# Routing the first image's tokens between the matmuls of the second image's convolution (convolution mixer and mixture of experts, float32)

## What is computed

```python
def _branch(x, w, d):                      # d in (1, 4, 8, 12), nine taps each
    f = conv(x, w, dilation=d); f = softmax over the nine taps, per pixel
    return sum over taps k of shift_k(x, d) * f[k]
def _L0_conv_ref(x, ...):
    cat = concatenate([x] + [_branch(x, w, d) for w, d in ...], axis=1)   # 1280 channels
    y = w_proj @ cat + b_proj
    return relu(_group_norm(y, gamma, beta))
def _moe(tokens, router_w, w1, b1, w2, b2):
    probs = softmax(tokens @ router_w.T)
    rw, re = top_k(probs, 2); rw = rw / rw.sum(-1)
    out = tokens
    for e in range(8):
        out = out + combine[:, e:e + 1] * (gelu(tokens @ w1[e] + b1[e]) @ w2[e] + b2[e])
    return out
x = x + _L0_conv_ref(_ln_c(x), ...)
t = _to_tokens(x)                          # 18432 tokens
t = t + _L0_ffn_ref(_ln_t(t), ...)
```

## Time and profile before

| | us |
|---|---|
| median of 3 runs (lowest to highest) | 2617.31 (2616.59 to 2630.79) |
| the profiled execution | 2616.45 |
| its span | 2614.6 |
| A0, A1 (17 to 247, 700 to 936) | 230, 236 |
| C0, C1 (313 to 700, 1002 to 1393) | 387, 391 |
| R (1393 to 1843) | 450 |
| experts (1843 to 2388) | 545 |
| output (2388 to 2615) | 227 |

### The profile page before, as it was taken

The page is one execution under the profiler, slowest core; times in us unless marked ns, Lnnn a source line. Parts: engine busy times, 40 slices in busy tenths (PEclk is TensorE's granted clock), DMA queues, the critical chain, the costliest instruction groups (busy, mean ns, idle before and its releaser), DMA issues.

```text
span 2614.6 us, 61081 instructions
## 1 busy us (share of the span) xinstructions
PE 2046.2 (78%) x20292; PEld 1918.8 (73%) x20293; DVE 1624.7 (62%) x4238; ACT 1187.8 (45%) x2441; POOL 1026.5 (39%) x1390
## 2 busy tenths in 40 slices
PE   5887699999688867999994766750799999995332
PEld 4777499999678757999993766650799999994222
DVE  3554475666555545656665867663577899885644
ACT  4654233333256533333333544440577777773211
POOL 4444012233234411223320677777455566563000
PEclk9999599999899977999996655555899999997555
DMA  4332156677433214656766897753566555555887
GB/s 122 91 88 68 47 174 157 158 179 176 123 85 85 79 43 132 170 142 170 174 160 186 277 325 264 257 189 131 164 195 206 172 162 159 150 158 177 289 296 271
DMA packets 328031, 434.91 MB, mean 166 GB/s; under 512 B 86586, under 2 KB 253114, under 8 KB 326778
## 3 DMA queue, kind: packets, MB, share of 16 engines
q1 hardware_dynamic: 273618, 315.07, 42.9%
q0 software_dynamic: 41024, 97.10, 10.7%
q10 hardware_dynamic: 13200, 20.19, 2.1%
HBM read 278.46 MB, written 159.94 MB: 168 GB/s over the span
## 4 chain that ended last, share of the span: by engine, by line
PE 46%; DMA 17%; POOL 15%; issue 10%; DVE 5%; ACT 4%; DVEq 2%; SPq 1%; POOLq 0%; ACTq 0%
PE ps_y L381 16%; POOL expert_in L1786 8%; DMA expert_out<-e_out,dest 7%; PE ps L381 6%; POOL taps L1752 6%; PE ps_o L854 6%; PE ps_a L381 5%; PE ps_b L790 5%; DMA o_y<-expert_out 3%; DMA o_acc<-res_scratch 2%; ACT g_rows L1059 2%; PE ps_f L762 2%; DMA expert_in<-c_ln,pos 2%; PE ps_o L841 1%; PE ps_x L967 1%
## 5 line engine op out<-in xcount | busy, mean ns | idle before, releaser
L381 PE MATMUL ps_y<-cat_hi,wp 128*128 128x288 f32 x2048 | 469.5, 305 | 1.8 <-DVE cat_lo L1370 1.8
L1774 POOL DMA_DIRECT2D patches<-rows_scratch x352 | 194.8, 598 | 651.5 <-PE ps_o L854 492.4
L1809 POOL DMA_INDIRECT expert_out<-e_out,dest x304 | 310.3, 1021 | 237.4 <-DMA expert_out<-e_out,dest 117.4
L1786 POOL DMA_INDIRECT expert_in<-c_ln,pos x288 | 294.4, 1022 | 186.8 <-DVE pos L1515 92.1
L381 PEld LDWEIGHTS ps_y<-cat_hi,wp 128*128 128x128 f32 x2048 | 343.2, 189 | 2.0 <-DVE cat_lo L1370 2.0
L1137 ACT ACTIVATE cat_hi<-ps_o 128x288 fp32r<-128x288 f32 (+1 forms) x576 | 200.1, 386 | 252.9 <-PE ps_o L854 164.2
L381 PE MATMUL ps_y<-cat_lo,wp 128*128 128x288 f32 x1024 | 301.4, 294 | 0.0
L1370 DVE SCALAR_TENSOR_TENSOR cat_lo<-ps_o,cat_hi 128x288 fp32r<-128x288 f32 (+1 forms) x576 | 219.4, 419 | 129.8 <-ACT cat_hi L1137 129.6
L1752 POOL TENSOR_TENSOR taps<-taps,g_rows 96x108 f32<-96x108 f32 (+1 forms) x432 | 200.7, 494 | 242.2 <-ACT g_rows L1059 238.5
L381 PE MATMUL ps<-e_hi,w_now 128*128 128x256 f32 x1216 | 243.8, 284 | 1.2 <-issue 1.1
L381 PE MATMUL ps<-w,h_hi 128*128 x1216 | 234.5, 291 | 5.6 <-DVE h_lo L1658 5.6
(11 more groups left out here) (181 smaller groups left out, 4774.1 us busy)
## 6 DMA issues: line engine op xcount, KB each, us to landing
e_x<-expert_in SPq DMA_DIRECT2D x152, 260.0 KB
o_y<-expert_out SPq DMA_DIRECT2D x48, 768.0 KB, 5.3
patches<-rows_scratch SPq DMA_DIRECT2D x160, 192.0 KB
patches<-rows_scratch SPq DMA_DIRECT2D x256, 108.0 KB
patches<-rows_scratch SPq DMA_DIRECT2D x192, 112.0 KB
x_in<-in_x SPq DMA_DIRECT2D x48, 384.0 KB, 3.3
rows_scratch<-rows_st SPq DMA_DIRECT2D x48, 384.0 KB, 3.1
y_scratch<-y_acc SPq DMA_DIRECT2D x16, 1152.0 KB, 11.6
```

The costliest lines, as they stand in the source:

```text
L381: mm = eng.matmul(out, lhs[p], rhs[q], start=start and n == 0, stop=stop and n == 2)
L1774: pool.dma_start(patch_target(s, n), patch_source(m, s, n)).then_inc(patch_pooled[s % RING], 16)
L1786: pool.indirect_dma_start(out=xs_dram, out_offset=bass.IndirectOffsetOnAxis(ap=at, axis=0), in_=c_ln[:, v, k // TT, k % TT], in_offset=Non ...
L1809: pool.indirect_dma_start(out=ys_dram, out_offset=bass.IndirectOffsetOnAxis(ap=at, axis=0), in_=e_out[:, u, j], in_offset=None).then_inc(e ...
```

## The change

Image 0's part of R is done inside C1, one tile of 128 tokens at a time, in **slots** between the units; R then handles only image 1, 12 pairs. Slots lie at unit n = 1 of each step (at n = 2 in kind 1 of the classes), and at n = 5 of kind 3 as well: 79 slots, of which 72 take a tile and 12 rank a pair. To make room:

- `ps_b` has one bank instead of two, and a band matrix is made in two halves (`band(s, 0)`, `band(s, 1)`), the second one at n = 1 of the step before, in both images. The bank that is free, `ps_k`, takes one transposed tile, six tiles' router products and the counts.
- The ring of patches has three buffers instead of four (RING), in both images. In C1 POOL begins 6 of 18 patch loads in kind 3 and none in strips; SP begins the others.
- SP also loads image 0's x and y in C1 (24 blocks, 48 loads) and stores 72 tiles of the residual; POOL does image 0's additions x + y (24) and its 144 scatters, three per step.
- The router products are taken from the tile before normalisation (x as the stationary operand), and mean and deviation are put in on VectorE with the sum of the router's rows.
- Six constants are loaded at the program's start and not in R; image 0's group norm is done at the start of A1, image 1's in R. In R the expert weights, biases and fills are begun after the second pair's loads and not halfway.
- EARLY goes from 30 to 28.

```diff
-RING = 4
+RING = 3
-EARLY = 30
+EARLY = 28
...
-            ps_b = psum(r1, "ps_b", [128, 2, 512])
+            ps_b = psum(r1, "ps_b", [128, 512])
+            ps_k = psum(r1, "ps_k", [128, 512])
...
+        slot_ticks = []
+        for s_ in range(1, STEPS):
+            first = 2 if kind(s_) == 1 and s_ > UNITS1 else 1
+            slot_ticks += [unit(s_) + first] + ([unit(s_) + 5] if kind(s_) == 3 else [])
+        slot_of_tick = {u: k for k, u in enumerate(slot_ticks)}
...
+        ROUTE_AT, RANK_AT = TP - 1, TP + 2
...
-        def second_queue(s, n):
-
+        def second_queue(m, s, n):
+
+            if m:
+                return n % 3 == 2 and kind(s) == 3
             return n % 2 == 1 if kind(s) == 3 else kind(s) == 0 and n >= 6
```

SP in C1, and in R:

```diff
+                if m:
+                    sp.wait_ge(y_stored, 16 * 8)
+                    load_block(0)
+                    load_block(1)
+                blocks, kept = 2, 0
                 for s in range(STEPS):
+                    while m and blocks < ITILES // TT and slot_step(3 * blocks - 4) + 3 <= s:
+                        load_block(blocks)
+                        blocks += 1
+                    while m and kept < ITILES and slot_step(kept) + 4 <= s:
+                        store_residual(kept)
+                        kept += 1
                     load_patches(s)
...
+            load(0, 0)
+            load(1, 1)
+            sp.dma_start(etiles[:], a["k_etiles"]).then_inc(consts_in, 16)
+            sp.dma_start(w_stage[:].rearrange("p e c -> p (e c)"), a["w1"]).then_inc(w_loaded, 16)
```

PE:

```diff
+                def turn_tile(t):
+
+                    j, k = divmod(t, TT)
+                    pe.wait_ge(r_x1, j + 1)
+                    for c in range(CC):
+                        pe.transpose(ps_k[:, c * 128:(c + 1) * 128], r_x[:, j % 2, c, k * 128:(k + 1) * 128], ident[:])
+                    for c in range(CC):
+                        mm = pe.matmul(ps_k[:, 256 + t % TP * E:256 + (t % TP + 1) * E], r_x[:, j % 2, c, k * 128:(k + 1) * 128],
+                                       router[:, c], start=c == 0, stop=c == CC - 1)
+                    mm.then_inc(r_tok, 1)
...
+                def slot(k):
+
+                    after(pe, r_resd, min(k, ITILES))
+                    after(pe, r_read, min(k // TP, CPAIRS))
+                    after(pe, r_based, max(0, min((k - RANK_AT + TP - 1) // TP, CPAIRS)))
+                    if k >= RANK_AT and (k - RANK_AT) % TP == 0 and k < RANK_AT + ITILES:
+                        rank_pair((k - RANK_AT) // TP)
+                    if k < ITILES:
+                        turn_tile(k)
...
                 for s in range(STEPS):
                     if s + 1 < STEPS:
-                        band(s + 1)
+                        band(s + 1, 0)
                     for n in range(CC * parts(s)):
                         branch(s, n // parts(s), n % parts(s))
+                        k = slot_at(m, s, n)
+                        if k is not None:
+                            slot(k)
                         if s and n in (1, 3):
                             project(s - 1, n // 2, 0)
                             project(s - 1, n // 2, 1)
+                        if n == 1 and s + 1 < STEPS:
+                            band(s + 1, 1)
```

ScalarE (norm_tile normalises one tile from ps_k into r_ln, deviate is the square root of one tile's variance, relu_block group norm and ReLU of a block of three tiles):

```diff
                     for n in range(CC * parts(s)):
                         cat(s, n // parts(s), n % parts(s))
+                        if n == 1 and s + 1 < STEPS:
+                            band_hi(s + 1, 1)
+                        t = slot_at(m, s, n, 1)
+                        if t is not None and t < ITILES:
+                            norm_tile(t)
+                            if t % TT == 1 and (t + 2) // TT < ITILES // TT:
+                                relu_block((t + 2) // TT)
+                        k = slot_at(m, s, n)
+                        if k is not None and k < ITILES:
+                            deviate(k)
```

VectorE (moments: statistics of ps_k; tile_factors: reciprocal and factor after the root; residual: ps_k + r_ln, after which the bank is free; choose: 19 operations in six parts; place: 7 in three):

```diff
                 for s in range(STEPS):
                     if s + 1 < STEPS:
-                        band_lo(s + 1)
+                        band_lo(s + 1, 0)
                     for n in range(CC * parts(s)):
                         split(s, n // parts(s), n % parts(s))
+                        t = slot_at(m, s, n, 2)
+                        if t is not None and t < ITILES:
+                            residual(t)
+                        if n == 1 and s + 1 < STEPS:
+                            band_lo(s + 1, 1)
+                        for part in range(6):
+                            p = pair_at(m, s, n, ROUTE_AT, 2 + part)
+                            if p is not None:
+                                choose(p, part)
+                        for part in range(3):
+                            p = pair_at(m, s, n, RANK_AT, 2 + part)
+                            if p is not None:
+                                place(p, part)
+                        k = slot_at(m, s, n)
+                        if k is not None and k < ITILES:
+                            moments(k)
                         if n in (1, 3):
                             adds(s - 1, n // 2)
+                        if k is not None and k < ITILES:
+                            tile_factors(k)
```

POOL:

```diff
                 for s in range(STEPS):
-                    shared = [n for n in range(loads(s)) if second_queue(s, n)]
+                    while m and blocks < ITILES // TT and slot_step(3 * blocks - 2) + 2 <= s:
+                        add_block(blocks)
+                        blocks += 1
+                    while m and quarters < 4 * CPAIRS and placed_step(quarters // 4) + 3 + quarters % 4 <= s:
+                        scatter_rows(quarters // 4, quarters % 4)
+                        quarters += 1
+                    shared = [n for n in range(loads(s)) if second_queue(m, s, n)]
```

More of the change, by code:

```diff
@@ L534, in _ @@
             sp.dma_start(wg_stage[:], a["w_gen"]).then_inc(consts_in, 16)
+            for dst, src in ((same[:], a["k_same"]), (router[:], a["router"]), (order[:], a["k_order"]),
+                             (before[:], a["k_before"]), (region[:], a["k_region"]), (token[:], a["k_token"])):
+                sp.dma_start(dst, src).then_inc(consts_in, 16)
             leave(sp)
@@ L626, in _ @@
+            with sp.Fori(1, CPAIRS // 2) as t:
+                for v in range(2):
+                    load(t * 2 + v, v)
+                    store(t * 2 + (v - 2))
+            store(CPAIRS - 2)
             sp.wait_ge(cw_lo, 1)
             sp.dma_start(w_stage[:].rearrange("p e c -> p (e c)"), a["w2"]).then_inc(w_loaded, 16)
-            store(PAIRS - 1)
+            store(CPAIRS - 1)
             for u in range(2):
-                wait(sp, c_stored[u], 16 * PAIRS)
+                wait(sp, c_stored[u], 16 * CPAIRS)
@@ L790, in show, with band @@
                     return pe.matmul(out, sel[:, b, 3 * y + x], pixels, start=True, stop=True, skip_group_check=True)
-                def band(s):
+                def band(s, j):
                     b = kind(s)
-                    after(pe, band_done, m * STEPS + s)
-                    for j in range(2):
-                        bank = ps_b[:, j]
+                    after(pe, band_done, 2 * (m * STEPS + s) + j)
+                    for bank in (ps_b,):
                         for y in range(3):
@@ new lines, in norm_tile @@
+                def norm_tile(t):
+                    p = t // TP
+                    act.wait_ge(r_factor, t + 1)
+                    if t % TP == 0 and p >= HELD:
+                        act.wait_ge(r_scattered[p % HELD], 16 * TP * TOP * (p // HELD))
+                    act.activation(r_ln[:, p % HELD, t % TP, 0:C], ps_k[:, 0:C], ACT.Identity,
+                                   bias=r_nmr[:, p % 2, t % TP:t % TP + 1], scale=r_rstd[:, p % 2, t % TP:t % TP + 1]).then_inc(r_lnd, 1)
+                if m:
+                    act.wait_ge(gn_dve, 9)
+                    relu_block(0)
@@ new lines, in residual @@
+                def residual(t):
+                    dve.wait_ge(r_lnd, t + 1)
+                    after(dve, r_stored[t % 3], 16 * (t // 3))
+                    dve.tensor_tensor(r_res[:, t % 3], ps_k[:, 0:C], r_ln[:, t // TP % HELD, t % TP, 0:C],
+                                      ALU.add).then_inc(r_resd, 1)
+                every = lambda z: z.unsqueeze(2).broadcast_to([128, TP, E])
+                ranks = order[:].rearrange("p (o e) -> p o e", o=1).broadcast_to([128, TP, E])
+                picked = [0]
@@ L1774, in _ @@
                         pool.dma_start(patch_target(s, n), patch_source(m, s, n)).then_inc(patch_pooled[s % RING], 16)
+                while m and quarters < 4 * CPAIRS:
+                    scatter_rows(quarters // 4, quarters % 4)
+                    quarters += 1
+                if m:
+                    for u in range(HELD):
+                        pool.wait_ge(r_scattered[u], 16 * TP * TOP * (CPAIRS // HELD))
                 leave(pool)
```

466 lines of the change are left out of this document (316 added, 150 removed).

## The result

The changed kernel took 2693.72 us (median of 4 runs, 2688.76 to 2700.53) beside 2621.75 for the kernel before on the same chip: ratio 1.0272, 95% interval 1.0229 to 1.0316, slower. The profiled execution took 2697.88 us, 81.4 more than that of before.

What follows compares the result with a forecast made beforehand. It took C1 as bound by PE time and R by POOL's scatters. From 2616.45 us, R -192.5, output +2, A1 +1, C0 +5 and C1 +239 gave 2671, rounded 2670 us; range 2575 to 2745, likeliest case 2630 to 2740.

Steps and rivals of the forecast that it cites:

- R, -192.5: Routing stage: 144 fewer scatters save 195 us, constants moved out save 3.5, later first scatter costs 6.
- C1, +239: Second image's convolution: start 5, strips 29, slots 113, ReLUs 22, `seen` 14, choice 36, clock 20 us more.
- The strip's loop: C1 strips: each tile waits through the engines in turn, 7.4 us a strip against 5.50; chance 0.58.
- rival (1): C1: throughput decides, the loop hides behind PE's projections; 2497 us, or 2585 with half the stalls hidden; chance 0.22.
- rival (2): C1: choice and ReLUs fall wholly into VectorE's waits, -50 us, 2603 to 2630; chance 0.12.
- The order at n = 1: C1: VectorE reaches the second half band before the tile's statistics; e1 was expected to regain 27 + 51 us.
- rival (5): C1 classes: patches come late, PE waits 2 us in one class of three, +10 us; inside the loop's 0.58.
- The clock, +20: C1: PE, with gaps in its work, runs partly below 2.4 GHz, costing 20 us.
- rival (3): C1: PE's clock falls in every leg, time 2740 to 2840 us; chance 0.08.
- C0, +5: First image's convolution: halved bands and three patch buffers use up its loop's slack, +5 us (0 to 10).
- Output and experts: Output stage: EARLY 28 makes one more pair load its residual there, +2 us (0 to 6); experts had no term.
- rival (4): C1: each of POOL's 24 additions keeps VectorE out of a chain operation, +47 us, 2717; chance 0.05.

Runs made afterwards that it cites:

- e4: Changed kernel with each of a pair's 17 chained choice operations on VectorE issued twice; 2719.70 us, ratio 1.0381 to the kernel before.
- e5: e2 with GpSimd's patch loads ahead of its addition and scatters, and SP's residual stores one step earlier; 2625.48 us, ratio 1.0005 to the kernel before.
- e1: Changed kernel with a tile's statistics, additions, factors and square root ahead of the second half band on VectorE and ScalarE; 2655.04 us, ratio 1.0134.
- e2: Changed kernel with a tile's statistics, factors, normalising and residual all in its slot's tick, ahead of the second half band; 2658.53 us, ratio 1.0169.
- e3: Changed kernel with GpSimd's patch loads of a step begun ahead of that step's addition and scatters; 2680.11 us, ratio 1.0232.
- e8: Changed kernel with six added PE products of 128 columns at five places of each class, output wrong; 2723.93 us, ratio 1.0381.
- e6: Kernel before with three patch buffers in place of four; 2665.37 us, ratio 1.0162.
- e9: e5 with each row class's two stores of the finished image cut into four; 2768.27 us, ratio 1.0094, on a slower chip.
- e11: Kernel before with three patch buffers and the finished image's stores cut into four; 2757.93 us, ratio 1.0061, on a slower chip.

## Why the prediction was right, term by term

- **R, -192.5; measured -189.1.** The scatters took 197.3 us from first to last for 144, 192.7 less (forecast 195.0). The start, from C1's last addition to the first scatter, grew by 3.6 (+6 less 3.5 forecast). Right.
- **C1, +239; measured +243.9.** The first strip begins 2.6 us later (5), the strips took 42.7 more (29, and 7 for ReLUs), the classes 198.6 more (113 for slots, 15 ReLUs, 14 `seen`, 36 choice, 20 clock: 198). The strip's loop in the chain is the forecast's list; PE is busy for 79% of C1 (70 forecast), VectorE for 59%, so throughput, rival (1), does not decide, and choice isn't hidden (e4), as rival (2), a draw, wanted. e5 shows it from the other side: the same work in another order took 69 us less.
- **The parts of C1 are less right than its sum; that the sum agrees to 5 us is in part luck.** The order at n = 1 is worth 41 us (e1), where I expected 78; with the whole tile in its slot's tick, which ends PE's wait for the residual too, it is 32 (e2). Other things stood just behind: PE's own products in e1's strips, SP's loads in e2's and e5's strips (I had put SP's strip at 7.4 us and held it hidden), GpSimd's queue and the patches in the classes. So taking the loop away doesn't bring back the 142 us that I gave to the slots. Late patches were not in the 239, and the clock, below, may be more than its 20: terms too small stood beside one too large. Choice is about half on the path (e4), as forecast. With all orders mended, e5's C1 is still 175 us longer than before: PE is busy for 103 us more of it, and what the other 70 or so are wasn't taken apart.
- **Late patches, rival (5), +10.** Its mechanism is there, and behind the loop its price: 12 us (e3). Once the loop is mended it is larger: e5's three orders together gave 69 us where e2 and e3 gave 32 and 12.
- **The clock, +20, rival (3).** PE had 1.2 GHz for 164 of C1's 626 us, in 32 stretches. The time of the 1536 `ps_y` products (counted once where they overlap), before and after, and twelve of them in two strips:

```profile
998.20:1380.70 382.50, 235.00 (x1536) 208.84 (x1536) 0.98 0.64 162
1020.30:1646.70 626.40, 272.69 (x1536) 244.63 (x1536) 0.87 0.61 175
...
1040.83:1043.91 3.08, 3.08 (x16) 2.93 (x16) 0.00 (x0) 0.00 (x0) 0.00 (x0) 0.50 0.47 133
1073.40:1075.10 1.70, 1.70 (x20) 1.63 (x20) 0.78 (x3) 0.00 (x0) 0.00 (x0) 1.00 0.58 174
```

  331 of the products took over 0.4 us instead of 7: the granted clock fell in places, not in every leg, so (3) at 2740 and over was wrong. The 38 us are PE's busy time. Of the 198 us that PE's work holds in the chain of C1, 82 lie at 1.2 GHz; with 3.08 us for what takes 1.70 at the full clock, the path has at most some 37 us of the clock by estimate, less where something else ends right behind. So 20 may be too small by up to 17; no run settled it (e8).
- **C0, +5; measured +20.4.** This step failed in size, outside its 0 to 10. Four late classes (20.4 to 23.2 us) hold 18 of the 20.4 us, and the halved bands some 3. I priced a step's slack in PE's loop and not the store that SP stands in, 6.0 to 7.8 us in the kernel before too, which four buffers covered and three don't (e6: +41 us for the kernel before in both stages; e9, e11: C0 at 390).
- **Output and experts.** The output took 8.8 us more (2 forecast). All variants of the changed kernel on the first chips have 234.6 to 239.1 there; e6, which keeps EARLY 30, 233.8 and before 228.5. So some 5 of the 8.8 come without any change to that stage; EARLY wasn't tested by itself. The experts' -4.3 wasn't forecast.
- **GpSimd's addition, rival (4).** It took 1.81 us (2 forecast). VectorE's residuals took 0.418 us in the mean while one ran and 0.416 elsewhere, but they read PSUM, and I found no choice operation beside an addition, so the rival got no test.

Against 54 us forecast the profiled execution grew by 81: C0 15, the output 7, C1 5, R 3 and the time ahead of C0 2 more than said, the experts 4 and A1's head 1 less. The medians give 72.

## What to carry to other kernels

Before work is put into the gaps of a full engine, follow one item of it through every in-order queue, from slot to slot: the sum of that loop, not of each engine's work, told the size here, if with help from errors that cancelled. When the loop is found, look at the queues that stand right behind it (here SP's issues and GpSimd's loads behind scatters): mending one order gave 10 to 40 us, all of them together 70. A buffer given up for room costs what it covered: look for the longest time that the loading queue ever stands, here in a store once every four classes.

## What was not expected of the hardware

An issue can hold its queue: the second of two 1152 KB stores back to back held SP for 5.9 to 11.2 us in the changed kernel, while each of four 576 KB stores with patch loads between them took 0.4 to 0.9. The first of two took 0.4 as well, and at the end of C0, where the four pieces follow each other at once, they took 0.4, 0.7, 2.1 and 2.0 (e9): SP stands at a store right behind another, and size alone doesn't tell for how long. Two whole stores with loads between them weren't tried. And chips differ: the kernel before took 2618 to 2624 us in three comparisons and 2740 in two on other chips, and 144 scatters 197 us on the one kind and 243 on the other. The scatters themselves are no slower there: GpSimd was busy with the 144 for 152 us on both (changed kernel and e9). The time is in waits, in part for releasers that the profile can't name; why stays open. So the same edit is worth another ratio there.
